# Attention scores of a language-model tower: from seven bfloat16 part products to three float32r part products, two heads side by side on TensorE's rows

## What is computed

```python
h = emb[x]                                    # x: 2 x 2048 tokens, 256 features
Q, K, V = (heads(w, b) for w, b in ...)       # 16 heads of 16 features each
score = jnp.einsum('bhsd,bhtd->bhst', Q, K) / jnp.sqrt(jnp.float32(D_K))
attn = jax.nn.softmax(score, axis=-1)
o = jnp.einsum('bhst,bhtd->bhsd', attn, V)
h = o.transpose(0, 2, 1, 3).reshape(B, S, D_MODEL) @ wo + bo
```

## Time and profile before

| | us |
|---|---|
| median of 3 runs | 3943.44 |
| the profiled execution, as timed | 3942.12 |
| its span in the trace | 3940.3 |
| projection | 0 to about 130 |
| attention, first maxima alone | 150 to 228 |
| attention, 30 chunks with maxima beside them | 228 to 1615 |
| attention, last two chunks | 1615 to 1684 |
| the stages behind it, not edited | 1685 to the end |

### The profile page before, as it was taken

One profiled execution on the slowest core, in us unless ns is written; L12 is line 12 of the kernel. 1 busy time (PEld: TensorE's weight loads), 2 busy tenths in 40 slices (PEclk: granted clock), 3 DMA queues, 4 the chain that ended last, 5 costly groups with the idle time before them and its releaser, 6 DMA issues. The chain is left out here.

```text
span 3940.3 us, 64166 instructions
## 1 busy us (share of the span) xinstructions
PE 3642.9 (92%) x20577; PEld 1970.5 (50%) x20577; DVE 2970.8 (75%) x3944; ACT 2765.8 (70%) x3830; POOL 1451.6 (37%) x1284
## 2 busy tenths in 40 slices
PE   7699999999999999945899999999999999996999
PEld 4223333233323333222677767777777777775554
DVE  5799999899989999333778888888888888886111
ACT  2246666666666666812888999999888989996232
POOL 3000000000000000000677877777777877786000
PEclk9789999999999999977999999999999999998999
DMA  5510101010100100042011111111111111113221
GB/s 136 150 42 4 41 4 41 4 42 16 30 22 23 38 7 4 5 138 81 33 44 55 60 55 55 59 63 53 52 47 54 60 55 55 49 55 102 81 92 49
DMA packets 121702, 202.32 MB, mean 51 GB/s; under 512 B 25392, under 2 KB 68368, under 8 KB 121456
## 3 DMA queue, kind: packets, MB, share of 16 engines
q1 hardware_dynamic: 101264, 173.97, 13.7%
q10 hardware_dynamic: 18656, 20.85, 1.7%
q0 software_dynamic: 1536, 4.20, 0.7%
HBM read 147.83 MB, written 50.72 MB: 50 GB/s over the span
## 5 line engine op out<-in xcount | busy, mean ns | idle before, releaser
L1047 POOL TENSOR_TENSOR m_g<-m_hs,m_cb 128x512 f32<-128x512 f32 x1024 | 1295.4, 1280 | 379.3 <-DVE m_hs L1322 376.3
L661 DVE TENSOR_REDUCE a_mx<-a_ps_m 128x1 f32<-128x512 f32 x2048 | 1311.8, 686 | 156.4 <-PE a_ps_m L520 139.2
L632 ACT ACTIVATE a_probs<-a_ps_s 128x1024 f32<-128x1024 f32 x1024 | 995.0, 1020 | 466.5 <-PE a_ps_s L557 465.9
L1322 DVE TENSOR_TENSOR_SCAN m_hs<-m_da,m_carry,m_ps_x 128x512 f32<-128x512 f32 x768 | 967.8, 1274 | 177.8 <-PE m_ps_x L1118 157.1
L1248 ACT ACTIVATE m_da<-m_delta,m_a_cur 128x512 f32<-128x512 f32 x1024 | 734.0, 717 | 102.1 <-DVE m_hs L1322 101.2
L520 PE MATMUL a_ps_m<-a_k,a_q 112*128 112x512 bf16 x2048 | 732.0, 394 | 41.9 <-DMA a_q<-q_scr 26.5
L1233 ACT ACTIVATE m_bu<-m_dut,m_bt 128x512 f32<-128x512 f32 x1024 | 730.8, 714 | 0.2
L1118 PEld LDWEIGHTS m_ps_x<-m_ident,m_bu 128*128 128x128 f32 x4096 | 494.6, 144 | 383.4 <-issue 302.0
L1118 PE MATMUL m_ps_x<-m_ident,m_bu 128*128 128x128 f32 x4096 | 635.0, 278 | 41.8 <-DVE m_hs L1322 28.8
L1130 PE MATMUL m_ps_y<-m_ident,m_g 128*128 128x128 f32 x4096 | 625.5, 276 | 14.0 <-POOL m_g L1047 14.0
L557 PE MATMUL a_ps_s<-a_q,a_k 115*128 115x512 bf16 (+1 forms) x2048 | 611.3, 381 | 1.4
(11 more groups left out here) (154 smaller groups left out, 2461.4 us busy)
## 6 DMA issues: line engine op xcount, KB each, us to landing
m_cb<-c_scr SPq DMA_DIRECT2D x128, 512.0 KB, 3.7
y_scr<-m_ysb SPq DMA_DIRECT2D x16, 1024.0 KB, 6.7
ffn_y<-y_scr SPq DMA_DIRECT2D x16, 1024.0 KB, 10.2
a_k<-k_scr SPq DMA_DIRECT2D x224, 64.0 KB, 2.2
a_q<-q_scr SPq DMA_DIRECT2D x224, 64.0 KB, 2.6
m_xn<-xn_scr SPq DMA_DIRECT2D x16, 512.0 KB, 5.1
q_scr<-p_partsq SPq DMA_DIRECT2D x24, 256.0 KB, 2.4
k_scr<-p_partsk SPq DMA_DIRECT2D x24, 256.0 KB, 2.6
```

The lines of the kernel that those rows point to most:

```text
L632: nc.scalar.activation(probs[:, t % 2, 2 * half:2 * half + 2], ps_s[half][:, :, :], ACT.Exp, scale=float(DK) ** -0.5).then_inc(exped, 1)
L661: nc.vector.reduce_max(mx[:, i // NC, i % NC:i % NC + 1], bank(i), AX.X).then_inc(m_maxed, 1)
L1047: nc.gpsimd.tensor_tensor(g[:, t % NG], hs[:, t % NHS], cb[:, quarter % 2, n % CQ], ALU.mult).then_inc(g_ok, 1)
L1322: nc.vector.tensor_tensor_scan(hs[:, t % NHS, rev], da[:, t % NDA, rev], ps_x[:, t % NX, rev], carry[:, n, i:i + 1] if p else 0.0, ALU.mul ...
```

## The change

The parts are float32r instead of bfloat16: two parts hold a value, and three products of parts give a score. A stack is 3 x 16 = 48 rows (50 with the two parts of the maximum), so two heads fit on TensorE's 128 rows: one at rows 0 to 63, one at 64 to 127.

- Projection: ACT writes the high part straight from PSUM; DVE makes the low part with one operation for each 512 columns (bias added, high part subtracted). The four splitting operations, `full` and `rest` are gone. Two parts of 4 bytes are stored instead of three of 2.
- PE pairs one score product with one maximum on the other half of the rows; `HEADS = [1, 0, 3, 2]` sees to it that the halves differ. The order in a step is: (score, maximum) four times, then `values`. A pair's first product carries the waits of both.
- Banks: `ps_m` has four instead of three, `ps_s` three single ones instead of two double ones. So ACT's exponentials are 64 of 128 x 512 in a chunk instead of 32 of 128 x 1024.
- DVE takes the maxima of a round of four banks with three operations: one bank, two banks at once (128 x 1024 to 128 x 2), one bank.
- The negated maximum is turned by PE in float32, in item 14 of a chunk, into a bank of `ps_s`; ACT copies it out twice (once rounded), POOL makes the low part with one operation, SP writes four rows instead of three.
- Loads for a group: 24 transfers of 128 KB instead of 56 of 64 KB. The chunks inside a group are written out instead of looped.

```diff
-PARTS = 3
-Q_PART = [0, 0, 1, 1, 0, 2, 1]
-K_PART = [0, 1, 0, 1, 2, 0, 2]
+HP = HG // 2
+PARTS = 2
+Q_PART = [0, 0, 1]
+K_PART = [0, 1, 0]
...
-                            nc.scalar.activation(full[a][:, m], ps_qk[a][:, m], ACT.Identity,
-                                                 bias=b_col[a][:, m:m + 1]).then_inc(full_ok[a], 1)
+                            nc.scalar.activation(parts[a][:, buf, 0, m], ps_qk[a][:, m], ACT.Identity,
+                                                 bias=b_col[a][:, m:m + 1]).then_inc(high_ok[a], 1)
...
+                            last = nc.vector.scalar_tensor_tensor(
+                                out=parts[a][:, buf, 1, m], in0=ps_qk[a][:, m], scalar=b_col[a][:, m:m + 1],
+                                in1=parts[a][:, buf, 0, m].bitcast(FP32), op0=ALU.add, op1=ALU.subtract)
+                        last.then_inc(parts_ok[a], 1)
...
+        SR, MR = 3, 4
+        ps_s = pb("a_ps_s", [P, SR, CH], FP32)
+        ps_m = pb("a_ps_m", [P, MR, CH], FP32)
...
+                def max_score(buf, c, i):
+                    pair, st, tc, half = i // 32, i // 8 % 4, i // 2 % 4, i % 2
+                    row = half * (P // 2)
+                    nc.tensor.matmul(ps_m[:, i % MR], q_st[row:row + KQ, buf, c, pair, st * P:(st + 1) * P],
+                                     k_st[row:row + KQ, buf, pair, tc * CH:(tc + 1) * CH],
+                                     start=True, stop=True).then_inc(m_scored, 1)
...
+                def turned_score(buf, c, t, h):
+                    row = h % 2 * (P // 2)
+                    nc.tensor.matmul(turned(HG * t + HEADS.index(h)), k_st[row:row + KQM, buf, h // 2, t * P:(t + 1) * P],
+                                     q_st[row:row + KQM, buf, c, h // 2], start=True, stop=True).then_inc(scored, 1)
...
                     for t in range(NT):
+                        for j in range(HG):
+                            i = HG * t + j
+                            if i == NEG and with_neg:
+                                pe.wait_ge(exped, ONE + e * ITEMS + NEG - SR + 1)
+                                transpose_neg(e + 1)
+                            if m_buf is not None:
+                                if m_buf != buf and i % 32 < 2:
+                                    pe.wait_ge(loaded[m_buf][2 * (i // 32) + i % 2], ONE + loads)
+                                max_free(e + AHEAD, i)
+                            turned_free(e, i, with_neg)
+                            turned_score(buf, c, t, HEADS[j])
+                            if m_buf is not None:
+                                max_score(m_buf, m_c, i)
                         if t > 0 or v_buf is not None:
+                            pe.wait_ge(exped, ONE + e * ITEMS + HG * t)
                             if t == 1:
                                 pe.wait_ge(o_copied, ONE + e)
                             values(v_buf if t == 0 else buf, (t - 1) % NT)
...
-                            nc.scalar.activation(probs[:, t % 2, 2 * half:2 * half + 2], ps_s[half][:, :, :], ACT.Exp,
-                                                 scale=float(DK) ** -0.5).then_inc(exped, 1)
+                            nc.scalar.activation(probs[:, t % 2, HEADS[j]], turned(i), ACT.Exp, scale=float(DK) ** -0.5).then_inc(exped, 1)
...
-                        nc.vector.reduce_max(mx[:, i // NC, i % NC:i % NC + 1], bank(i), AX.X).then_inc(m_maxed, 1)
+                    for r in range(BLK // MR):
+                        for b, wide in ((0, 1), (1, 2), (3, 1)):
+                            i = MR * r + b
+                            dve.wait_ge(m_scored, ONE + m * BLK + i + wide)
...
+                            nc.vector.reduce_max(mx[:, i:i + wide], ps_m[:, b:b + wide], AX.X).then_inc(m_maxed, 1)
```

More of the change, by code:

```diff
@@ L6 @@
 FP32 = mybir.dt.float32
-BF16 = mybir.dt.bfloat16
+F32R = mybir.dt.float32r
 I32 = mybir.dt.int32
@@ L93, in embed_and_project @@
         hT = sb("p_hT", [P, 2, KD, CH], FP32)
-        full = [sb(f"p_full{n}", [P, KD, CH], FP32) for n in "qk"]
-        rest = sb("p_rest", [P, KD, CH], FP32)
-        parts = [sb(f"p_parts{n}", [P, 2, PARTS, KD, CH], BF16) for n in "qk"]
+        parts = [sb(f"p_parts{n}", [P, 2, PARTS, KD, CH], F32R) for n in "qk"]
         ps_t = pb("p_ps_t", [P, KD, CH], FP32)
@@ L402, in load @@
                     for h in heads:
+                        first, pair = h % 2 * (P // 2), h // 2
                         for stack, scr, part in ((k_st, k_scr, K_PART), (q_st, q_scr, Q_PART)):
@@ L498, in body @@
                         stage_v(g + 1, 1 - buf)
-                    with pool.Fori(AHEAD, NC if last else NC + AHEAD) as c:
-                        split(g * NC + c)
+                    with pool.Fori(1, NC if last else NC + 1) as c:
+                        low(g * NC + c)
                 groups(pool, body)
@@ L504, in _ @@
             def _(pe):
-                def max_blocks(m, buf, c, first, end, loads=None):
-                    for i in range(first, end):
-                        h, st, tc = i // 16, i // 4 % 4, i % 4
-                        if i % 16 == 0 and loads is not None:
-                            pe.wait_ge(loaded[buf][h], ONE + loads)
-                        before = item(i) - 3
-                        if before == NEG:
-                            pe.wait_ge(neg_t, ONE + m)
-                        elif before > NEG:
-                            pe.wait_ge(m_maxed, ONE + m * BLK + before + 2)
-                        elif before >= 0:
-                            pe.wait_ge(m_maxed, ONE + m * BLK + before + 3)
-                        else:
-                            pe.wait_ge(m_maxed, ONE + m * BLK + (1, 2, 0)[i])
-                        nc.tensor.matmul(bank(i), q_st[0:KQ, buf, bass.ds(c, 1), h, st * P:(st + 1) * P].rearrange("p c n -> p (c n)"),
-                                         k_st[0:KQ, buf, h, tc * CH:(tc + 1) * CH],
-                                         start=True, stop=True).then_inc(m_scored, 1)
@@ new lines, in max_score, with max_blocks @@
+                def max_score(buf, c, i):
[4 more added lines that the diff above has]
+                                     start=True, stop=True).then_inc(m_scored, 1)
+                def max_blocks(m, buf, c, first, end, loads):
+                    for i in range(first, end):
+                        if i % 32 < 2 and loads is not None:
+                            pe.wait_ge(loaded[buf][2 * (i // 32) + i % 2], ONE + loads)
+                        max_free(m, i)
+                        max_score(buf, c, i)
@@ new lines, in transpose_neg, with turned_free @@
+                def transpose_neg(m):
+                    pe.wait_ge(neg_ok, ONE + m + 1)
+                    nc.tensor.transpose(ps_n, neg[:, :], ident32[:, :]).then_inc(neg_ps, 1)
+                def turned_free(e, i, with_neg):
+                    q = slot(i) - SR
+                    if q >= 0:
+                        if q == NEG and with_neg:
+                            pe.wait_ge(neg_h, ONE + e + 2)
+                        else:
+                            pe.wait_ge(exped, ONE + e * ITEMS + (q if q <= NEG else q - 1) + (q != NEG))
+                    elif not isinstance(e, int) or e:
+                        pe.wait_ge(exped, ONE + e * ITEMS + min(0, q + 2))
@@ L601, in body @@
                     else:
-                        with pe.Fori(NC - AHEAD, NC) as c:
+                        for c in range(NC - AHEAD, NC):
                             chunk(g, buf, c, buf, 1 - buf, c - (NC - AHEAD), True)
                 groups_first(pe, body)
-                pe.wait_ge(exped, ONE + G * NC * NT * 2 + 2)
+                pe.wait_ge(exped, ONE + G * NC * ITEMS)
                 values(1, NT - 1)
```

202 lines of the change are left out of this document (75 added, 127 removed).

## The result

The changed kernel takes 3922.5 us (median of 14 runs, 3906.1 to 3932.8), the kernel before 3944.2 (14 runs, 3937.5 to 3947.5). The ratio is 0.994, 95% interval 0.9927 to 0.9953: faster by 22 us, where 55 had been forecast. The direction was right, less than half of the size came. The 14 runs of the changed kernel lie in two groups some 20 us apart (six from 3906.1 to 3912.5 us, seven from 3926.4 to 3932.8, one at 3918.5); the profiled one, 3912.5, is of the shorter group, so its stages add up to more gain (29.6 us) than the medians show (22).

What follows compares the result with a forecast made beforehand. PE was taken as the bound, DVE 8% behind. Steady chunks -66, last two chunks +14, first maxima -2, projection -1 sum to -55 us: 3888 us on the median, range 3720 to 4010.

Steps and rivals of the forecast that it cites:

- What bounds it; the loop: Steady step: PE bounds the old kernel; with three score banks a PE-ACT loop of 2.38 us plus weight loads sets the new.
- Its size: Steady step in the 30 chunks: 2.38 + 0.30 = 2.68 us, 43.5 us a chunk against 45.7, -66 us.
- the third of the three weight loads: Steady step: the load of item 3's maximum, one of three exposed float32r loads taken at 0.10 us each.
- the 0.6 for turning and copying: Each chunk: 0.6 us added to 16 steps, for turning the negated maximum in item 14 and for copying out.
- DVE's round: Steady step: DVE's three operations over four maximum banks, 2.34 us (2.40 at most), against 2.40 before.
- Loads hidden: Rival, steady step: float32r loads cost nothing or are drawn ahead; step 2.38 us, time 3737 us; chance 20%.
- one after the other: Rival, steady step: score and maximum products of a pair don't run side by side; PE needs 2.92 us, 3998 us; chance 12%.
- more passes: Rival, products: a float32r product takes more than one pass; step 3.10 us, 4101 us, or some 4550; chance 12%.
- The clock falls: Rival, steady step: PE's idle time lowers the clock to 1.2 GHz; step 4.0 us, 4250 us for half the chunks; chance 7%.
- last two chunks +14: Last two chunks, without maxima: 83 us against 69.2, so 14 us longer.
- the first maxima -2, the weight transposes 0: Before the attention: maxima alone gain 2 us by DVE's shorter round; transposes between them stay under DVE's pace, costing 0.
- 2.58 a step: Last two chunks: step of 2.58 us, since no maximum stands behind item 3, against 2.68 in the steady chunks.

Runs made afterwards that it cites:

- the filled chunks: The changed kernel with a product, its result unused, issued beside each score product in the last two chunks: 3888.9 us, ratio 0.987.

## Why the prediction was right and wrong

**What bounds it; the loop.** Right, and shown by the halves of `values` and by the exchanged banks: three banks and `values` in the queue make a loop through PE and ACT; PE waits for ACT, not DVE, in the fourth item.

**Its size.** 2.61 us instead of 2.68. The links as measured: product with its load 0.50, hand-over 0.03, exponential 0.60, back 0.05, then 0.43 to `values` and 1.00: 2.61. The step that was mis-sized is the third of the three weight loads: since the two products of a pair run side by side, their two loads do too, and one is paid. That each load costs 0.10 was right (0.11: the product behind a wait takes 0.50, the others 0.39). 16 x 2.61 + 0.6 is 42.4, as the ruler says, so the 0.6 for turning and copying was right. The 30 chunks gave -88.8. Their steady 42.4 would have given 30 x -3.3 = -99. But the first four and the last two of the 30 take 43.9 to 48.5 us, 14 us more in all than six steady ones, with steps of 2.70 to 2.77 us (the first also has the clock at 0.50 until 263 us); of the same six in the kernel before only the first was longer, 46.2. In the program they stand outside the loop, with waits against constants; whether that is the cause wasn't tried. The two chunks at the loop's return, which the prediction had no term for, give 4 us back: 8 and 8 us above the steady chunk before, 4 and 7 now. DVE's round was sized right: alone it takes 2.33 us (forecast 2.34), in a step with a rest behind it 2.42.

The Trainium skill, "TensorE: Matmul & The Clock Gate", section "LDWEIGHTS (loading the stationary operand)", has a weight load take the number of columns divided by 1.2 in ns, which is 107 ns for 128. The trace agrees for float32r, 0.11 us. By the section "Weight-path perf modes" of the same page of the Trainium skill the fast weight load is off for FP32; with its 0.11 us, where a bfloat16 load added 0.01 at most, float32r behaves here as that section has FP32.

**Loads hidden**, **one after the other**, **more passes**: all three out. The exposed load is seen; a pair starts within 0.01 us, and with the pairs on one half the step is 2.85; a product takes 0.39 us.

**The clock falls.** This rival was put at the wrong place. It was priced for the steady steps, and they kept 1.00. The step of the sum that failed was "last two chunks +14" and "the first maxima -2, the weight transposes 0": they measured +44 and +21, and both took the clock for granted. The earlier trace rows had it at 0.51 right behind the first block, and the same trace has 1.00 only for the 20 us in which the transposes were made, which no row of mine showed. For the last chunks 2.58 a step was near what the filled chunks take (2.61 and 2.67), so +18 of +44 was the mechanism that the prediction had, and 26 the clock. For the first maxima I reasoned from DVE's pace as if the transposes' 0.60 were PE's at any clock. At 0.50 a maximum and two transposes take PE 1.03 to 1.34 us, DVE's operation 0.60, and PE is the bound.

**The range and the chances.** 3720 to 4010 held the time. The forecast's own range, 3850 to 3930, held it too. But 3922 lies in it by luck, by two misses of opposite sign, 23 us more gain in the 30 chunks and 53 more loss in the two stretches. A time inside the range is no evidence for the sum.

## What to carry to other kernels

In a ring of N buffers, count the items between two long pieces of work in the producer's queue, not the place of the piece: if there are more than N, one of them waits through the whole round trip; shortening the piece helps, moving it doesn't. Where the change makes products smaller or rarer, read the granted clock of every stretch that has them alone, ends and starts too, and price each at both levels: here 170 us outside the steady chunks took back three quarters of what 1300 us inside them gave. And where a run fits a rival's number, ask first whether it could have fitted the theory's.

## What the runs showed of the hardware

- Two float32r products of 512 columns on the two halves of TensorE's rows start 0.01 us apart and take 0.39 us each, as one bfloat16 product does. A product for an idle half starts ahead of one that stands before it in the queue and waits for the other half (both scores at 1002.16, both maxima at 1002.50, queued score, maximum, score, maximum).
- The same edit in rows (112 or 115 to about 50) kept the clock from rising at the start (0.50 instead of 1.00 from 170 to 190 us) and didn't make it fall at the end (1.00). A second product on the idle half kept it up at the end and didn't lift it at the start. Single half-row products with the loop's gaps ran on at 1.00 for 5 to 68 us before it fell to 0.50, in seven profiles.
- A float32r weight load of 128 columns that nothing covers adds 0.11 us (0.50 instead of 0.39); for a pair on the two halves it is paid once.
- A maximum over two banks takes DVE 1.21 us, against 0.69 for one; in the pace of a round that is 0.06 us less than two single ones, and nothing of it reached the time.
